# Output projection and FFN base layer as seven half-size products (Strassen's scheme) over two pairs of batch elements

## The chip, the core and the metric

The kernel runs on one core of a Trainium2 chip. A core has five engines with a queue each: TensorE (PE, with its weight loads shown apart as PEld), VectorE (DVE), ScalarE (ACT), GpSimd (POOL) and SyncE (SP), which here issues every DMA. Engines wait for each other through semaphores only, and each works through its own queue in order. The metric is the device time of one execution in microseconds (us).

## The reference, cut to what matters

```python
# x is [32, 64, 1024]: 2048 tokens of 1024 features; all in float32
x = x + attn(cond(x))                 # attn ends with: return y @ w_proj.T
c = conv1d(x)(9 taps, 4 groups) + ctx + bias
base   = c @ W_base.T + b_base
logits = c @ W_router.T               # 8 experts, the top 2 taken
h      = einsum('td,erd->ter', c, A)  # 8 experts x rank 16
lora   = einsum('ter,te,eor->to', h, w, B) * SCALING
x = x + base + lora
```

`cond` mixes the 64 channels of each batch element with weights that an MLP makes for it. Attention is over 64 tokens with 32 heads of 32, a causal mask and a ten-token prefix.

## The kernel before

Every wide product is done in FP32R, TensorE's one-pass form of float32. To keep the precision, each operand is split into a high and a low part (`hi` by a copy on ACT, `lo = raw - hi` by a subtraction on DVE), and a product is three passes: hi*hi, hi*lo, lo*hi (`split_passes`). The tokens are 16 pairs of batch elements (`NP`), 128 tokens each.

- **Attention** (`unit_step`) runs over 8 head groups `g` of 128 columns times 4 units `u` of 512 tokens, 32 units. In a unit `n = 4g + u` PE does the scores of the unit before (`attend_scores`, L774), turns that unit's values (`turn_values`, L834, which waits for `vT_copied`), projects K, Q and V (L822), turns the probabilities of the unit before between Q and V (`attend_transposes`, L783 and L790), and ends with `attend_values` of the unit before (L799, L805). DVE does the softmax of the unit before, the rotation of K and Q, and in a unit with `u == 0` three small operations that end in `avbd` (L1409), which waits for `attend_values` (`y_mm`). ACT copies V out of PSUM (`vT`, L1122) when V's projection is done. With `u == 3` the next group's q/k/v weights are split (`w_st`, `w_hi`, `w_lo`; L1020, L1189). The attention's output goes to DRAM (`y_scratch`).
- **Output and FFN stage** (`pair_step`) takes one pair after another. For a pair PE does the output projection of pair p+2 (`project_out`, L882: 8 chunks x 3 passes x 2 halves of 512 columns = 48 matmuls), the FFN's last layer of pair p (`last_layer`, L909: 8 x 3 x 3 = 72 matmuls of 388 or 384 columns, for 1024 base, 128 adapter and 8 router columns), a transpose (L919), the convolution of pair p+1 (`convolve`, L894: 16 matmuls in float32, 32 records), and the low-rank term (`low_rank`, L929: 9 matmuls). DVE adds the residual (L1283), puts the router together and writes the output; POOL adds the bias (L745). Between projection and convolution the pair goes through DRAM once (`x_scratch`, L672 and L681).
- The order on each engine is that of the code: written out by hand, with no scheduler. All weights of the stage are split once, near the end of attention (`wproj_hi`, `wffn_hi` and their `lo`).

## Time and profile before

| | us |
|---|---|
| median of 3 runs (lowest to highest) | 1203.87 (1201.65 to 1205.7) |
| the profiled execution | 1202.29 |
| its span | 1200.5 |
| PE busy | 1184.9 (99%) |
| DVE busy | 725.1 (60%) |
| ACT busy | 385.5 (32%) |
| POOL busy | 55.2 (5%) |
| DMA queue 1 | 84.32 MB, 20.9% of 16 engines |

The profile is of one execution, and its times count from the start of the span. Attention with its mixing stage takes the first 730 us or so, the output and FFN stage the rest. A busy share is an average over stages; a matmul's duration includes the time in which the next one already runs, so the pace of matmuls is read from the distance between starts, not from durations.

### The profile page before, as it was taken

The page shows a single profiled execution, that of the slowest core. Times are in us where ns is not written, and L with a number is a line of the kernel's source. Part 1 is how long each engine was busy: PE and PEld are TensorE (multiplying, and loading weights), DVE is VectorE, ACT ScalarE, POOL GpSimd, SP SyncE. Part 2 cuts the span into 40 slices and gives each one's busy share as a digit, 9 for nine tenths or more (in the row PEclk, how much of TensorE's full clock was granted, in tenths as well). Part 3 has the DMA queues.
Part 4 walks back from the last instruction along what each step waited for, and adds up shares of the span by engine and source line. Part 5 has one row for each costly group of instructions (what it writes and reads, how often), then busy time and mean ns, then how long its engine had stood idle before and what let it go on. Part 6 is the DMA issues. An engine that isn't in the chain of part 4 may idle for free.

```text
span 1200.5 us, 19493 instructions
## 1 busy us (share of the span) xinstructions
PE 1184.9 (99%) x7936; PEld 1032.0 (86%) x7936; DVE 725.1 (60%) x1484; ACT 385.5 (32%) x702; POOL 55.2 (5%) x25
## 2 busy tenths in 40 slices
PE   6999999999999999999999999999999999999998
PEld 5988888888888888888888888899999999999998
DVE  5887767677777777768768598633333333333333
...
PEclk9999999999999999999999999999999999999999
...
GB/s 255 126 37 70 10 19 62 10 19 62 20 9 68 13 9 72 9 12 69 9 57 24 150 97 187 126 90 90 91 90 90 92 107 92 91 90 90 108 73 54
DMA packets 58679, 85.56 MB, mean 71 GB/s; under 512 B 5963, under 2 KB 44767, under 8 KB 57695
## 3 DMA queue, kind: packets, MB, share of 16 engines
q1 hardware_dynamic: 58590, 84.32, 20.9%
...
## 4 chain that ended last, share of the span: by engine, by line
PE 96%; DVE 2%; issue 1%; POOL 0%; ACT 0%; SPq 0%; DMA 0%; DVEq 0%
PE psum L822 44%; PE psum L909 17%; PE psum L882 13%; PE psum L894 4%; PE psum L774 3%; PE psum L805 3%; PE psum L790 2%; PE psum L929 2%; PE psum L252 2%; PE psum L834 2%; PE psum L843 1%; PE psum L783 1%; PE psum L799 1%; DVE z L345 0%; POOL f_x1b L745 0%
## 5 line engine op out<-in xcount | busy, mean ns | idle before, releaser
L822 PE MATMUL psum<-z,w_hi 128*128 128x512 f32 x1536 | 481.7, 395 | 0.0
L822 PEld LDWEIGHTS psum<-z,w_hi 128*128 128x128 f32 x1536 | 282.4, 188 | 55.5
L822 PE MATMUL psum<-z,w_lo 128*128 128x512 f32 x768 | 300.1, 391 | 0.0
L822 PEld LDWEIGHTS psum<-z,w_lo 128*128 128x128 f32 x768 | 144.1, 188 | 31.5
L1091 ACT ACTIVATE a_kbd<-a_kr 32x512 f32<-32x512 f32 x128 | 80.8, 631 | 225.6 <-DVE a_kr L1207 224.5
L745 POOL TENSOR_TENSOR f_x1b<-f_x,_bbase 128x1024 f32<-128x1024 f32 x16 | 50.4, 3153 | 1072.8 <-DVE a_aprob L1257 690.3
L1221 DVE TENSOR_TENSOR a_prob<-psum,a_mask 128x512 f32<-128x512 f32 x64 | 44.0, 687 | 86.0 <-PE psum L774 86.0
L909 PE MATMUL psum<-f_wfhi,f_chi 128*128 128x384 f32 (+1 forms) x360 | 85.7, 339 | 0.6 <-DVE f_clo L1313 0.6
L909 PE MATMUL psum<-f_wflo,f_chi 128*128 128x384 f32 (+1 forms) x360 | 85.5, 338 | 0.0
L909 PE MATMUL psum<-f_wfhi,f_clo 128*128 128x384 f32 (+1 forms) x360 | 85.3, 338 | 0.0
L1327 DVE COPY f_lg<-psum 128x8 f32<-128x8 f32 x16 | 2.7, 168 | 130.2 <-PE psum L909 130.2
L882 PE MATMUL psum<-f_wphi,f_yhi 128*128 128x512 f32 x240 | 74.5, 391 | 0.7 <-ACT a_ysb L1040 0.7
L882 PE MATMUL psum<-f_wplo,f_yhi 128*128 128x512 f32 x240 | 74.2, 390 | 0.0
L882 PE MATMUL psum<-f_wphi,f_ylo 128*128 128x512 f32 x240 | 74.0, 390 | 0.0
L909 PEld LDWEIGHTS psum<-f_wfhi,f_chi 128*128 128x128 f32 x360 | 65.1, 188 | 2.1 <-issue 1.0
L1283 DVE TENSOR_TENSOR f_x<-psum,f_xt 128x1024 f32<-128x1024 f32 x14 | 28.8, 2054 | 63.0 <-PE psum L882 59.5
L909 PEld LDWEIGHTS psum<-f_wfhi,f_clo 128*128 128x128 f32 x360 | 64.9, 188 | 0.0
L909 PEld LDWEIGHTS psum<-f_wflo,f_chi 128*128 128x128 f32 x360 | 64.8, 188 | 0.0
L1073 ACT ACTIVATE f_rs<-f_rs 128x1 f32<-128x1 f32 x16 | 3.3, 204 | 179.8 <-DVE f_rs L1330 179.8
L894 PE MATMUL psum<-_toep,_x 128*128 128x128 f32 x512 | 59.8, 275 | 0.0
L1133 ACT ACTIVATE a_vbd<-psum 64x256 f32<-64x256 f32 x128 | 48.7, 381 | 33.8 <-PE psum L834 32.6
L894 PEld LDWEIGHTS psum<-_toep,_x 128*128 128x128 f32 x512 | 58.5, 192 | 1.2
...
## 6 DMA issues: line engine op xcount, KB each, us to landing
w_st<-in_wqkvT SPq DMA_DIRECT2D x7, 1536.0 KB, 6.9
m_x<-in_x SPq DMA_DIRECT2D x16, 512.0 KB, 4.2
y_scratch<-a_ysb SPq DMA_DIRECT2D x32, 256.0 KB, 2.5
f_yst<-y_scratch SPq DMA_DIRECT2D x16, 512.0 KB, 4.4
f_xt<-in_x SPq DMA_DIRECT2D x16, 512.0 KB, 3.6
x_scratch<-f_x SPq DMA_DIRECT2D x16, 512.0 KB, 2.6
_x<-x_scratch SPq DMA_DIRECT2D x128, 64.0 KB, 2.6
out<-f_osb SPq DMA_DIRECT2D x15, 512.0 KB, 2.8
```

The lines of the kernel that those rows point to most:

```text
L252: mm = pe.matmul(slot_bank(i, c // 4)[:, (c % 4) * P:(c % 4 + 1) * P], xbuf[i % NX][:, c * P:(c + 1) * P], aggT[:, i, :, :].rearrange("p b ...
L745: pool.tensor_tensor(x1b[:].rearrange("p (m q) -> p q m", q=PH), x1[:].rearrange("p (q m) -> p q m", q=PH), bbase[:].rearrange("p (m q) -> ...
L774: mm = pe.matmul(bS[2 * t + s // 2][NC * b:NC * b + NC, at:at + KW], qr[heads, (2 * s + b) * NC:(2 * s + b + 1) * NC], kbd[heads, 2 * s + ...
L805: mm = pe.matmul(y[2 * HD * hp:2 * HD * (hp + 1), (2 * s + b) * NC:(2 * s + b + 1) * NC], vbd[:, s, b, hp, :], pT[hp][:, s, NC * b:NC * b ...
L822: mm = pe.matmul(dst, w[:, c, x, :], zs, start=(c == 0 and i == 0), stop=(c == KC - 1 and i == 2))
L882: mm = pe.matmul(proj_banks(p)[n], y[:, c, :], w[:, c, n * 512:(n + 1) * 512], start=(c == 0 and i == 0), stop=(c == KC - 1 and i == 2))
L894: mm = pe.matmul(bC[:, o:o + P], x8[:, CONV * b + g, j:j + P], toep[:, g, j, :], start=(j == 0), stop=(j == 1))
L909: mm = pe.matmul(bF[:, at:at + n1 - n0], a[:, c, :], w[c][:, n0:n1], start=(c == 0 and i == 0), stop=(c == KC - 1 and i == 2))
L1091: cp = act.activation(kbd[HD * h:HD * (h + 1), :, h % 2 * NC:(h % 2 + 1) * NC], kr[HD * h:HD * (h + 1), :].rearrange("p (b k) -> p b k", k ...
L1133: cp = act.activation(vbd[NC * h:NC * (h + 1), :, b, :, HD * h:HD * (h + 1)], bV[NC * b:NC * (b + 1), :].rearrange("p (s a h e) -> p s a h ...
L1221: dve.tensor_tensor(prob[t][:].rearrange("p (s h) k -> p s h k", h=2), score_slots[:, UP * t:UP * (t + 1), 0:2 * NC].rearrange("p s (h k) ...
L1283: dve.tensor_tensor(x1[:].rearrange("p (q m) -> p m q", q=PH), bP.rearrange("p (m q) -> p m q", q=PH), xt[:].rearrange("p (m q) -> p m q", ...
```

## The change

Two pairs of batch elements (256 tokens) now make a group `G`. A product `Y = X W` of 256 tokens by 1024 by 1024 is cut into 2 x 2 blocks: X into blocks of 128 tokens by 512 features (A11, A12 of the first pair, A21, A22 of the second), W into blocks of 512 by 512. Strassen's scheme (in Winograd's form) makes the four blocks of Y from seven block products instead of eight: of A11, S1, A22, S2, A12, S4, S3, where S1 = A21+A22, S2 = S1-A11, S4 = A12-S2, S3 = A11-A21, with seven matching forms of W. Shares that several output blocks have in common are added by DVE (`shares`, `share21`, `share12`), or stay in the PSUM bank in which the next product adds to them.

- The stage has two phases: groups 0 to 7 do the output projection, groups 8 to 15 the FFN. Between them x plus bias goes through DRAM (`xn_scratch`). Groups 7 to 14 hold the two convolutions for the FFN group behind them.
- A product (`product`) is 4 chunks x 3 passes = 12 matmuls of 512 columns. The adapter and router columns (136 of them) are a product of their own (`hidden`, 2 pairs x 8 chunks x 3 passes = 48 matmuls of 136 columns), and the low-rank term is 12 matmuls of 512 columns.
- The seven forms of each weight matrix are made during attention: 16 preparations (`prep_at`), one in every unit with `u` 0 or 1 but the first, and one in unit 30. Each loads 1 MB of raw weights into the place of `w_st`, which is free then, makes four differences on DVE, splits seven parts of 256 columns (three copies on ACT, three subtractions on DVE), and stores 1.8 MB in `w_forms` in DRAM. A form in use (`wform`) is 2 MB; the four first ones are loaded in the last head group, the others behind it, and those of the FFN in group 7 (`turn_group`), each when group 7 has done the product that used its place.

The core of the diff:

```diff
 NF = L + NE * RANK + NE
+HALF, KH = L // 2, KC // 2
+NJ = NP // 2
+NPROD = 7
+A11, S1, A22, S2, A12, S4, S3, A21 = range(8)
+WEIGHT_SLOT = (0, 3, 4, 5, 1, 2, 6)
+B11, B21, B22, T1, T4, T2, T3 = range(NPROD)
+NPREP, PREP = 16, HALF // 2
...
-        def proj_banks(p):
-            return (bV, bQ) if p == 1 else (bQ, bK)
+            return bY if m < NG * NU - 1 else bS[3]
+        def prep_at(n):
+            g, u = n // NU, n % NU
+            if n == NG * NU - 2:
+                return NPREP - 1
...
+            def store_prep(k):
+                sp.wait_ge(prep_lo_set, 3 * (k + 1))
+                gemm, c, h = prep_part(k)
+                for part, s0, s1, src in ((0, 0, 5, prep_hi), (0, 5, 7, prep_hi_two), (1, 0, 7, prep_lo)):
+                    sp.dma_start(w_forms[gemm, s0:s1, :, part, c, PREP * h:PREP * (h + 1)].rearrange("s p n -> p s n"),
+                                 src[:].bitcast(F32)).then_inc(prep_out, 16)
+                sp.wait_ge(prep_out, 48 * (k + 1))
+            def load_form(gemm, i):
+                if gemm:
+                    sp.wait_ge(prod, NPROD * (NJ - 1) + i + 1)
+                sp.dma_start(wform[i][:].bitcast(F32), w_forms[gemm, WEIGHT_SLOT[i]]).then_inc(wform_in[i], 16)
...
             def unit_step(g, u):
+                n = NU * g + u
+                if n and prep_at(n - 1) is not None:
+                    store_prep(prep_at(n - 1))
+                if prep_at(n) is not None:
+                    load_prep(prep_at(n), u == 0 or n == 1)
                 if last(g):
...
+            def put_aside(G, t):
+                row_ready(G, t)
+                sp.dma_start(x1_dram[2 * G + t], x1[:, t, :]).then_inc(x1_out[t], 16)
+            def keep(G, t):
+                sp.wait_ge(xn_set, 2 * G + t + 1)
+                sp.dma_start(xn_dram[2 * G + t], xn[:, t, :]).then_inc(xn_out[t], 16)
...
+                load_ctx(p)
+                sp.wait_ge(x1_out[p % 2], 16 * (p // 2 + 1))
+                wait(sp, conv_mm, 2 * (p - 1) if p >= 2 else 0)
...
+            def turn_group():
+                G = NJ - 1
+                put_aside(G - 1, 0)
+                put_aside(G - 1, 1)
+                load_form(1, 0)
+                keep(G - 1, 0)
+                load_form(1, 1)
+                keep(G - 1, 1)
+                load_form(1, 2)
+                load_form(1, 3)
+                spread(2)
+                load_form(1, 4)
+                spread(3)
+                load_form(1, 5)
+                put_aside(G, 0)
+                load_form(1, 6)
+                put_aside(G, 1)
+                keep(G, 0)
+                load_x(G + 1, 0)
+                keep(G, 1)
+                load_x(G + 1, 1)
...
+            def product(G, i):
+                if G % NJ == 0:
+                    pe.wait_ge(wform_in[i], 16 * (G // NJ + 1))
+                pe.wait_ge(act_set, form_count(low_order, i, G))
+                if i == 0:
+                    wait(pe, row1_set, 2 * G - 1 if G else 0)
+                if i == 1:
+                    wait(pe, row1_set, 2 * G)
+                if i == 2:
+                    wait(pe, u21_set, G)
+                if i == 3:
+                    wait(pe, row2_set, G)
+                if i == 4:
+                    pe.wait_ge(s1_set, G + 1)
+                if i == 5:
+                    pe.wait_ge(u22_set, G + 1)
+                if i == 6:
+                    pe.wait_ge(w12_set, G + 1)
+                for c in range(KH):
+                    for n, (a, w) in enumerate(split_passes(act_hi[i], act_lo[i], 0, 1)):
+                        mm = pe.matmul(prod_bank[i][:], a[:, c, :], wform[i][:, w, c, :],
+                                       start=(i < 4 and c == 0 and n == 0), stop=(c == KH - 1 and n == 2),
+                                       skip_group_check=True)
+                mm.then_inc(prod, 1)
...
+            def hidden(G):
+                j = G - NJ
+                if j == 0:
+                    pe.wait_ge(wh_lo, 1)
+                wait(pe, hw_set, j)
+                for t, halves in enumerate(((A11, A12), (A21, A22))):
+                    for half, f in enumerate(halves):
+                        pe.wait_ge(act_set, form_count(low_order, f, G))
+                        for c in range(KH):
+                            for n, (a, w) in enumerate(split_passes(act_hi[f], act_lo[f], whhi, whlo)):
+                                mm = pe.matmul(bH[:, HIDDEN * t:HIDDEN * (t + 1)], a[:, c, :], w[:, KH * half + c, :],
+                                               start=(half == 0 and c == 0 and n == 0),
+                                               stop=(half == 1 and c == KH - 1 and n == 2))
+                mm.then_inc(hidden_mm, 1)
...
+            def group(G):
+                if ffn(G):
+                    hidden(G)
+                for i in range(4):
+                    product(G, i)
+                if ffn(G):
+                    turn_hidden(G)
+                if NJ - 1 <= G < 2 * NJ - 1:
+                    convolve(2 * (G - NJ + 1))
+                product(G, 4)
+                if NJ - 1 <= G < 2 * NJ - 1:
+                    convolve(2 * (G - NJ + 1) + 1)
+                product(G, 5)
+                if ffn(G):
+                    if G == NJ:
+                        pe.wait_ge(lora_lo, 1)
+                    pe.wait_ge(hwT_set, G - NJ + 1)
+                    low_rank(G, bA, 0, 0)
+                    low_rank(G, bC, 0, 1)
+                    low_rank(G, bD, 1, 2)
+                    pe.wait_ge(w12_set, G + 1)
+                    low_rank(G, bB, 1, 1)
+                product(G, 6)
+            for G in range(1, 2 * NJ):
+                group(G)
...
+            def prep_high(k):
+                act.wait_ge(prep_in, 32 * (k + 1))
+                wait(act, prep_out, 48 * k)
+                act.activation(prep_hi[:, 0:3, :], prep_raw[:, 0:3, :], ACT.Copy).then_inc(prep_hi_set, 1)
+                act.wait_ge(prep_sum, 4 * (k + 1))
+                act.activation(prep_hi[:, 3:5, :], prep_raw[:, 3:5, :], ACT.Copy).then_inc(prep_hi_set, 1)
+                act.activation(prep_hi_two[:], prep_raw[:, 5:7, :], ACT.Copy).then_inc(prep_hi_set, 1)
...
+            def first_share(G):
+                act.wait_ge(prod, NPROD * G + 1)
+                wait(act, v2_set, G)
+                act.activation(s1[:], bA[:], ACT.Copy).then_inc(s1_set, 1)
...
+                if prep_at(n) is not None:
+                    prep_high(prep_at(n))
+                if n == NG * NU - 1:
+                    for f in form_order(0):
+                        high(0, f)
                 act.wait_ge(mm_done[V_], n + 1)
                 wait(act, v_tr, n)
                 act.activation(vT[:], bV[:], ACT.Copy).then_inc(vT_copied, 1)
...
+            def prep(k):
+                dve.wait_ge(prep_in, 32 * (k + 1))
+                part = prep_raw
+                def take(dst, a, b, done):
+                    wait(dve, prep_sum, done)
+                    dve.tensor_tensor(part[:, dst, :], part[:, a, :], part[:, b, :], ALU.subtract).then_inc(prep_sum, 1)
+                take(T3, B22, T1, 0)
+                take(T1, T1, B11, 0)
+                take(T2, B22, T1, 4 * k + 2)
+                take(T4, B21, T2, 4 * k + 3)
+                for n, (s0, s1_, hi) in enumerate(((0, 3, prep_hi[:, 0:3, :]), (3, 5, prep_hi[:, 3:5, :]),
+                                                   (5, 7, prep_hi_two[:]))):
+                    dve.wait_ge(prep_sum, 4 * (k + 1))
+                    dve.wait_ge(prep_hi_set, 3 * k + n + 1)
+                    dve.tensor_tensor(prep_lo[:, s0:s1_, :], prep_raw[:, s0:s1_, :], hi.bitcast(F32), ALU.subtract
+                                      ).then_inc(prep_lo_set, 1)
...
+            def shares(G):
+                dve.wait_ge(s1_set, G + 1)
+                dve.wait_ge(x_in[0], 16 * (G + 1))
+                dve.tensor_tensor(w12[:], s1[:], x_of(G, 0)[:, HALF:L], ALU.add)
+                dve.wait_ge(x_in[1], 16 * (G + 1))
+                dve.tensor_tensor(u2[:], x_of(G, 1).rearrange("p (s n) -> p s n", s=2),
+                                  s1[:].rearrange("p (s n) -> p s n", s=1).broadcast_to([P, 2, HALF]), ALU.add
+                                  ).then_inc(v2_set, 1)
+                dve.wait_ge(v2_set, G + 1)
+                dve.wait_ge(prod, NPROD * G + 2)
+                dve.tensor_tensor(u2[:, 1, :], bC[:], u2[:, 1, :], ALU.add).then_inc(u22_set, 1)
...
+            def out_half(G, t, half, src, other):
...
                     dve.wait_ge(conv_mm, 2 * p + b + 1)
                     dve.tensor_tensor(
...
+                        raw[:, t, :, NC * b:NC * (b + 1)].rearrange("p q (g o) -> p g q o", g=CONV),
+                        bConv[:, 512 * b:512 * (b + 1)].rearrange("p (g q o) -> p g q o", g=CONV, q=PH),
+                        ctxb[t][:, b * NC:(b + 1) * NC].rearrange("p (g a o) -> p g a o", g=CONV, a=1)
                         .broadcast_to([P, CONV, PH, CG]), ALU.add).then_inc(conv_set, 1)
...
+                if prep_at(n) is not None:
+                    prep(prep_at(n))
+                if n == NG * NU - 1:
+                    first_forms()
...
+            def group(G):
+                if G:
+                    row2(G - 1)
+                    add_up(G, S3)
+                    low(G, S3)
+                if ffn(G):
+                    router(G)
+                shares(G)
+                if not ffn(G):
+                    share21(G)
+                if G < NJ - 1:
...
+                elif G < 2 * NJ - 1:
+                    share12(G)
+                    if ffn(G):
+                        split_hidden(G)
+                    convolved(2 * (G + 1 - NJ))
+                    low(G + 1, A11)
+                    low(G + 1, A12)
+                    convolved(2 * (G + 1 - NJ) + 1)
+                    low(G + 1, A22)
+                    low(G + 1, A21)
+                    add_up(G + 1, S1)
+                    add_up(G + 1, S2)
+                    low(G + 1, S1)
+                    out11(G)
+                    out12(G)
+                    if ffn(G):
+                        share21(G)
+                    add_up(G + 1, S4)
+                    low(G + 1, S2)
+                    low(G + 1, S4)
                 else:
-                    finish_last()
-                if ahead >= 2:
```

**ACT in a unit with `u == 0` (unit 4).** Before, in program order, from the copy of the turned probabilities to that of V's values (`a_vT`, `a_ysb` the attention's output, `a_vbd` V's blocks):

```order
L1032 ACTIVATE a_aT<-psum 128x512 [waits a_y_mm,a_a_tr]
L1035 ACTIVATE a_pT_106<-psum 128x512 [waits a_p_tr]
L1035 ACTIVATE a_pT_107<-psum 128x512 [waits a_p_tr]
L1114 ACTIVATE a_kbd<-psum 32x8x10 [waits a_scores,a_ak_tr]
L1114 ACTIVATE a_kbd<-psum 32x8x10 x3
L1122 ACTIVATE a_vT<-psum 128x512 [waits a_v_tr,a_v_mm]
L1040 ACTIVATE a_ysb<-psum 128x512 [waits a_y_out,a_y_mm]
L1133 ACTIVATE a_vbd<-psum 64x4x2x32 [waits a_y_mm,a_v_tr]
```

Now, the same place:

```order
L1146 ACTIVATE a_aT<-psum 128x512 [waits a_y_mm,a_a_tr]
L1149 ACTIVATE a_pT_110<-psum 128x512 [waits a_p_tr]
L1149 ACTIVATE a_pT_111<-psum 128x512 [waits a_p_tr]
L1223 ACTIVATE a_kbd<-psum 32x8x10 [waits a_scores,a_ak_tr]
L1223 ACTIVATE a_kbd<-psum 32x8x10 x3
L1160 ACTIVATE f_prep_hi<-f_prep_raw 128x768 [waits f_prep_out,f_prep_in]
L1162 ACTIVATE f_prep_hi<-f_prep_raw 128x512 [waits f_prep_sum]
L1163 ACTIVATE a_prep_hi_two<-f_prep_raw 128x512
L1236 ACTIVATE a_vT<-psum 128x512 [waits a_v_tr,a_v_mm]
L1154 ACTIVATE a_ysb<-psum 128x512 [waits a_y_out,a_y_mm]
L1247 ACTIVATE a_vbd<-psum 64x4x2x32 [waits a_y_mm,a_v_tr]
```

The three `prep` copies stand ahead of the copy of V, and the second of them waits for `prep_sum`, which DVE raises in four differences behind `avbd`.

**SP where the phases meet.** Before, in the stage's steady step (`f_yst` and `f_xt` are the inputs of a pair, `_x` the convolution's):

```order
L636 DMA f_xt<-in_x 128x1024 [waits f_x1_set]
L632 DMA f_yst<-y_scratch 128x1024 [waits f_y_lo]
L693 DMA out<-f_osb 128x1024 [waits f_out_set]
L628 DMA a_ctxb_122<-ctx_scratch 128x128 [waits f_conv_set]
L672 DMA x_scratch<-f_x_80 128x1024 [waits f_x1_set]
L681 DMA _x_91<-x_scratch 16x8x128 [waits f_conv_mm,f_x1_out]
L681 DMA _x_91<-x_scratch 16x8x128 x7
L636 DMA f_xt<-in_x 128x1024 [waits f_x1_set]
L632 DMA f_yst<-y_scratch 128x1024 [waits f_y_lo]
```

Now, from the load of the fifth FFN form in `turn_group` (`f_wform_53`) on; `x_scratch` takes x, `xn_scratch` takes x plus bias, `f_xn` is read back for FFN group 8:

```order
L682 DMA f_wform_53<-w_forms 128x4096 [waits f_prod]
L703 DMA f_ctxb_136<-ctx_scratch 128x128 [waits f_conv_set]
L760 DMA f_x_next<-x_scratch 16x8x128 [waits f_conv_mm,f_x1_out1]
L760 DMA f_x_next<-x_scratch 16x8x128 x7
L682 DMA f_wform_54<-w_forms 128x4096 [waits f_prod]
L746 DMA x_scratch<-f_x_126 128x1024 [waits f_row1]
L682 DMA f_wform_55<-w_forms 128x4096 [waits f_prod]
L746 DMA x_scratch<-f_x_126 128x1024 [waits f_row2]
L750 DMA xn_scratch<-f_xn 128x1024 [waits f_xn_set]
L699 DMA f_xn<-xn_scratch 128x1024 [waits f_row1,f_xn_out0]
L750 DMA xn_scratch<-f_xn 128x1024 [waits f_xn_set]
L699 DMA f_xn<-xn_scratch 128x1024 [waits f_v2,f_xn_out1] x2
```

Seven loads of 2 MB have come into the queue between the stores of the projection, and the reads of `f_xn` for group 8 wait for a store of `xn_scratch` to have landed.

**DVE in FFN group 8.** Behind the router, in program order (`f_w_84` and `f_u_85` hold the shares, `f_raw` the convolution's output, `f_act_lo` the low parts for group 9):

```order
L1428 TENSOR_TENSOR f_w_84<-f_s_83,f_xn 128x512 [waits f_x_in0,f_s1]
L1430 TENSOR_TENSOR f_u_85<-f_xn,f_s_83 128x1024 [waits f_x_in1]
L1435 TENSOR_TENSOR f_u_85<-psum,f_u_85 128x512 [waits f_prod,f_v2]
L1448 TENSOR_TENSOR f_w_84<-psum,f_w_84 128x512 [waits f_v2,f_prod]
L1547 TENSOR_TENSOR f_hwTlo<-psum,f_hwThi 128x256 [waits f_hwT_hi]
L1494 TENSOR_TENSOR f_raw<-psum,f_ctxb_135 128x4x8x16 [waits f_conv_mm,f_ctxb_in0]
L1494 TENSOR_TENSOR f_raw<-psum,f_ctxb_135 128x4x8x16 [waits f_conv_mm]
L1422 TENSOR_TENSOR f_act_lo_64<-f_raw,f_act_hi_56 128x512 [waits f_act_hi]
L1422 TENSOR_TENSOR f_act_lo_68<-f_raw,f_act_hi_60 128x512 [waits f_act_hi]
L1494 TENSOR_TENSOR f_raw<-psum,f_ctxb_136 128x4x8x16 [waits f_conv_mm,f_ctxb_in1]
L1494 TENSOR_TENSOR f_raw<-psum,f_ctxb_136 128x4x8x16 [waits f_conv_mm]
```

Before, this engine's convolution output stood behind the router with nothing between that waited for a DMA but `a_ctxb`. Now it stands behind two additions that wait for `x_in0` and `x_in1`, and the second convolution of a group on PE waits for the first one's output (`conv_set`).

## Rows read from the trace of the kernel before

**Rows 1.** The page: busy time, and the span in 40 slices.
```profile
PE 1184.9 (99%) x7936; PEld 1032.0 (86%) x7936; DVE 725.1 (60%) x1484; ACT 385.5 (32%) x702; POOL 55.2 (5%) x25
PEclk9999999999999999999999999999999999999999
```
**Rows 2.** Whom PE waited for: total us, times, longest.
```profile
PE psum L774 <- DVE a_avs L1404: 1.1, 1, 1.1
PE psum L882 <- ACT a_ysb L1040: 0.7, 1, 0.7
PE psum L909 <- DVE f_clo L1313: 0.6, 1, 0.6
```
**Rows 3.** Timeline of PE, one pair of the stage: start us, us, instruction.
```profile
906.46 0.69 PE L909 MATMUL psum<-f_wfhi,f_chi 128*128 128x384 f32 x3
...
919.14 0.63 PE L882 MATMUL psum<-f_wphi,f_yhi 128*128 128x512 f32 x2
...
923.37 3.73 PE L894 MATMUL psum<-_toep,_x 128*128 128x128 f32 x32
926.86 0.36 PE L929 MATMUL psum<-f_loraBhi,f_hwThi 128*128 128x248 f32 x1
927.06 0.28 PE L929 MATMUL psum<-f_loraBlo,f_hwThi 128*128 128x248 f32 x1
927.18 0.28 PE L929 MATMUL psum<-f_loraBhi,f_hwTlo 128*128 128x248 f32 x1
927.29 0.34 PE L929 MATMUL psum<-f_loraBhi,f_hwThi 128*128 128x388 f32 x1
...
928.34 0.63 PE L882 MATMUL psum<-f_wphi,f_yhi 128*128 128x512 f32 x2
```
**Rows 4.** Timeline of PE, in the pair before it.
```profile
899.64 0.62 PE L882 MATMUL psum<-f_wphi,f_yhi 128*128 128x512 f32 x2
```
**Rows 5.** Timeline of PE, end of unit 16 and unit 17.
```profile
410.92 1.24 PE L774 MATMUL psum<-a_kbd,a_qr 64*64 64x148 f32 x32
412.08 0.65 PE L834 MATMUL psum<-_ident,a_vT 128*128 128x128 f32 x4
423.50 0.60 PE L783 MATMUL psum<-_ident,a_aprob 128*128 128x128 f32 x4
```
**Rows 6.** Timeline of DVE there.
```profile
411.10 0.29 DVE L1409 TENSOR_TENSOR a_avbd<-a_avs,a_avh 128x128 fp32r<-128x128 f32 x1 [2.73 <-PE psum L805]
412.20 0.69 DVE L1221 TENSOR_TENSOR a_prob<-psum,a_mask 128x512 f32<-128x512 f32 x1 [0.81 <-PE psum L774]
416.66 0.33 DVE L1232 TENSOR_TENSOR a_atmp<-psum,a_astat 128x160 f32<-128x160 f32 x1
421.80 0.24 DVE L1257 CAST a_aprob<-a_aprob 128x160 fp32r<-128x160 f32 x1
433.00 0.69 DVE L1221 TENSOR_TENSOR a_prob<-psum,a_mask 128x512 f32<-128x512 f32 x1 [5.36 <-PE psum L774]
```
**Rows 7.** Timeline of ACT, units 16 and 17.
```profile
409.71 0.60 ACT L1122 ACTIVATE a_vT<-psum 128x512 f32<-128x512 f32 x1 [1.99 <-PE psum L822]
427.86 1.08 ACT L1035 ACTIVATE a_pT<-psum 128x512 f32<-128x512 f32 x2
```
**Rows 8.** DMA issues: what, times, KB each, median us from issue to landing.
```profile
w_st<-in_wqkvT SPq DMA_DIRECT2D x7, 1536.0 KB, 6.9
y_scratch<-a_ysb SPq DMA_DIRECT2D x32, 256.0 KB, 2.5
f_xt<-in_x SPq DMA_DIRECT2D x16, 512.0 KB, 3.6
out<-f_osb SPq DMA_DIRECT2D x15, 512.0 KB, 2.8
```
**Rows 9.** The loads of `f_wp_raw` (8 of 512 KB): issue on SP, landing.
```profile
L643 SPq DMA_DIRECT2D f_wp_raw<-in_wprojT x8: 432/448/876, 669.6 to 673.7; - x8
DMA to landing us min/median/max: 4.2/6.8/9.4
```
**Rows 10.** Timeline of DVE, the last operation.
```profile
1197.20 0.56 DVE L1372 TENSOR_TENSOR f_osb<-psum,f_x1b 128x388 f32<-128x388 f32 x1 [2.09 <-PE psum L929]
```

More of the change, by code:

```diff
@@ L391, in program, with at @@
[L391 to L395 removed]
+        FORM = 2 * KH * HALF * 4
+        def at(name, place, shape, dt=F32):
+            return Space(nc, "f", place).take(name, shape, dt)
+        acts_at, staged_at = zbase + 2 * Z, zbase + NU * Z
+        wide_at = staged_at + KC * 3 * P * 4
@@ new lines, in ffn_group @@
+            def ffn_group(G):
+                if G > NJ:
+                    store_out(G - 1, 1)
+                if G < 2 * NJ - 1:
+                    load_x(G + 1, 1)
+                if G < 2 * NJ - 2:
+                    spread(2 * (G - NJ + 2))
+                    spread(2 * (G - NJ + 2) + 1)
+                if G < 2 * NJ - 1:
+                    load_x(G + 1, 0)
+                store_out(G, 0)
+            for G in range(NJ - 1):
+                proj_group(G)
+            turn_group()
@@ L1453, in build @@
+            for G in range(2 * NJ):
+                group(G)
+ROUTE_EXP, ROUTE_ALL = 4, 16
 def build(nc, d, out):
```

805 lines of the change are left out of this document (393 added, 412 removed).

## The prediction

> **What bounds the kernel now.** I read the page first: PE is busy 99% of the span, and its granted clock is at full speed in all 40 slices, the higher of its two levels, 2.4 GHz [rows 1]. Then the waits of PE: behind the first 70 us they are single waits of about 1 us or less [rows 2]. So the path is PE's own queue, and what counts is the number of matmuls times their pace. The other question is whether DVE, ACT or SP, none of them full, now makes PE wait.
>
> Pace, from distances between starts: the last 30 matmuls of a projection take 906.46 - 899.64 = 6.82 us, 0.227 us for one of 512 columns [rows 3, 4]. The 72 of the last layer take 919.14 - 906.46 = 12.68 us (0.176 each). A low-rank matmul of 248 columns takes 0.115 (927.06 to 927.29 is two), all nine 1.48 (926.86 to 928.34), a convolution 926.86 - 923.37 = 3.49 [rows 3].
>
> **The change part by part.**
>
> *Matmuls, in 8 x two pairs.* Projection: 96 of 512 columns become 84: -12 x 0.227 = -2.7 us. FFN before: 2 x (12.68 + 1.48) = 28.3. After: 84 x 0.227 = 19.1, low rank 12 x 0.227 = 2.7, hidden columns 48 x (136 columns), together 21.8 + hidden. No row has a single pass of 136 columns. Lower bound: by columns from the 248-column row, 0.115 x 136/248 = 0.063. Upper bound: as slow per column as the float32 convolution, 3.49/16 = 0.218 for 128 columns, so 0.232. The nearest row is 248 columns at 0.115, and I take it: 48 x 0.115 = 5.5, FFN after 27.3, gain 1.0. Convolutions and transposes are the same. Sum: 8 x (2.7 + 1.0) = -29.7 us, with bounds of the hidden columns at -20 and +45 around it.
>
> That 248 columns take 0.115 where 136/248 would leave half says nothing yet of a floor. The Trainium skill (TensorE: Matmul & The Clock Gate, LDWEIGHTS) gives a weight load as its columns over 1.2 GHz, 107 ns for 128: by that the hidden matmuls go at 0.107 or more. The same page (Back-to-back issue gap) states about 81 ns for a sustained pair of load and matmul at 128 columns: by that hidden is 3.9 us a group, and the sum 13 us lower. The rows cannot tell these two apart.
>
> *Preparation in units with u = 0.* Seven of them (head groups 1 to 7). DVE's four differences stand behind `avbd`, which waits for the unit's last PE work and ends at 411.39 [rows 6]. One of 256 columns: between 0.33 (160 columns) and 0.69 (512) by column 0.43; the second does not depend on the first (0.34 from start to start), the others do: they end at about 413.1. ACT then makes two copies of 512 columns (two take 1.08, [rows 7]) and only then V's copy, 0.60. Without them V's copy is at 409.71, without a wait on PE's side. Now it ends near 413.1 + 1.0 + 0.6 = 414.8. PE turns the values at 412.08 [rows 5], and waits from there: 2.7 us. Queued behind it are K's, Q's and V's projections; nothing covers it. The three low-part subtractions (about 2.2 us) follow on DVE, so the softmax starts at 415.1 instead of 412.20, 2.9 later; since PE is 2.7 late itself and had 423.50 - 422.04 = 1.5 us to spare at the probabilities [rows 5, 6], nothing is added. Price 7 x 2.7 = 18.9. Bounds: 2.2 each (differences overlapping) to 3.2.
>
> *Preparation in units with u = 1 (8) and unit 30.* DVE is idle 5.36 us before the next softmax [rows 6], the work is 3.9. ACT is free from 428.9 [rows 7]. Hidden, cost 0, as long as the raw weights have landed: SP stores 1.8 MB in 1 KB pieces, waits for it to land, then loads 1 MB. At the pace of the single large load, 1.57 MB in 6.9 us less a fixed 1.6 (`y_scratch`: 0.26 MB in 2.5, so 1.6 fixed at 0.3 MB/us, [rows 8]), 0.3 MB/us, that is 7.7 + 5.1 us from 415 on, landing near 428; needed at about 430.5. Two us more per unit and V's copy is late: up to +16.
>
> *End of attention.* The first group's forms, 2.8 us of sums and 4.6 of low parts on DVE, push the last softmax to about its limit; there are the same four or five short waits as before [rows 2]. +1, between -1 and +4. The forms 4 to 6 land before they are used.
>
> *Projection groups.* PE 84 x 0.227 = 19.1 us. DVE, by operations of 512 columns at 0.65 to 0.98, 15.3, and no wait of PE has less than 1.5 us to spare. DMA is 4.2 MB in 19.1 us. Cost 0.
>
> *The turn, groups 7 and 8.* Time from the start of group 7. PE: group 7 with two convolutions lasts 26.1. Group 8: hidden to 31.6, products 0 to 3 to 42.5, transposes and a convolution to 46.4, product 4 to 49.1, then the second convolution. That waits for `conv_set` of the first, DVE's work behind `shares(8)`, which waits for x of both pairs from `xn_scratch`. SP issues these reads last in `turn_group`, each behind a store that must have landed, and the queue ahead holds from 2.7 us on seven forms of 2.1 MB, three stores and two spreads of 0.5 MB, some 17 MB. Rate: eight queued loads of 0.52 MB took from 669.6 to 673.7 + 9.4 = 683.1 [rows 9]; less the fixed 1.6 that is 4.19 / 11.9 = 0.35 MB/us; I take 0.365, since the first issues were not queued. Form 6 ends at 52, the store of group 7's last x and of `xn` at 55, landed 56.7; read x0 (3.6, [rows 8]) 60.4, store, landed 61, read x1 64.6. Then DVE: shares, one hidden part and the convolution's output, 4.6: 69.2. PE waits 69.2 - 49.1 = 20 us. Bounds: at 0.41 MB/us 15, at the single load's 0.30 30; and 0, if a small store does not have to wait behind the forms. The landing times of rows 9, from 4.2 for the shortest to 9.4, the more that is queued, speak for one queue in order; I take 20. The Trainium skill (DMA: Bandwidth & Descriptors, Queues, rings and completion order) says that on each DMA engine the descriptors of a ring are consumed in order, which rows 9 bear out.
>
> After 20 us without work PE may come back at the lower clock, 1.2 GHz; no row shows it there. Nothing to one convolution's 3.5 us; I take half, 1.7.
>
> *FFN groups 9 to 15.* 34.8 us each on PE; DVE's chain (router, shares, two convolution outputs, four low parts) ends about 5 us ahead of the next hidden product. Cost 0.
>
> *The end.* Before, one subtraction of 388 columns, 0.56 [rows 10], and a store of part of a row. Now two additions of 512 columns (1.3 us) and a store of 512 KB, 2.8 [rows 8]: 1.3 + 2.8 = 4.1 against 1200.5 - 1197.2 = 3.3, so +0.8; with the longer issue I take +1 (0 to 1.5).
>
> *Sum* against the profiled execution, 1202.3 (span 1200.5 and 1.8 around it): -29.7 + 18.9 + 1 + 20 + 1.7 + 1 = +12.9, 1215.2. The median of the runs shown is 1.6 above that execution: 1216.8, **1217 us**.
>
> **The rivals.**
> - *The small stores and reads pass the forms (or these move faster), so that the turn costs nothing.* Then 1217 - 21.7 = 1195.5. For it: the DMA engines are at a fifth of their time over the span. Against it: rows 9. 10%.
> - *V's copy is not held up, only the turn is.* 1217 - 18.9 = 1198. Against it: ACT works in order, and the order rows have the copies ahead. 5%. Neither of the two: 1177, 7%.
> - *The hidden columns go by the column, at 0.063 (the 248-column row scaled), or between that and 0.115*: up to 48 x 8 x 0.052 = 20 us less, 1197, 12%; half of it on the faster side. The other way, at 0.232: 1262, 4%. By the 81 ns that the Trainium skill's TensorE page (Back-to-back issue gap) states it would be 1204.
> - *The weights in 1 KB pieces come late in the units with u = 1*: 8 x 1.8 = +14, 1231, 9%. The price starts once store and load together take over 16 us.
> - That the change does not do what it says is not a case: seven products of 12 matmuls stand in the order.
>
> **How the numbers follow.** The forecast has 50%, its own range 1209 to 1229; the last 3% is spread. What this kernel's measurement can tell from no change is about 0.3%, 3.6 us. Faster than 1200.3: the turn free alone, neither wait, V's copy free alone and half of the fast hidden columns, 10 + 7 + 5 + 6 = 28%. Within: 8%, the other half and the low edge of the forecast. Slower: 64%. The range from 1193 to 1234 leaves out the case with neither wait, the slow hidden columns and some of the tails.
>
> **What would show it.** In the profile after: about 84 matmuls of 512 columns per group at 0.227; L999 in place of L882 and L909; the distance of the hidden matmuls, 0.115; seven waits of PE at the turning of V, 2.7 us each, on ACT's copy, none with u = 1; one wait of some 20 us of PE ahead of a convolution in FFN group 8, with DVE idle on a DMA to `f_xn` and the DMA engines full for 50 us before it; no PE wait over 1 us in groups 1 to 6 and 9 to 15. The forecast is wrong if the seven waits are below 1 us, if `f_xn` lands before product 4 of group 8 ends, or if PE waits in each group.

## The result, and the profile after

| | before | after |
|---|---|---|
| median, us (lowest to highest, 4 runs each) | 1204.78 (1201.65 to 1207.39) | 1247.12 (1242.56 to 1252.09) |
| the profiled execution, its span | 1202.29, 1200.5 | 1246.03, 1244.2 |
| mean granted clock | 1.000 | 0.979 |

The change makes the kernel slower: ratio 1.0353, 95% interval 1.0305 to 1.0402. The forecast was slower too, but 1217 us with a range up to 1234, 30 us short.

The page after, against [rows 1]: fewer matmuls, but PE is no longer full, and its clock is not either. In the slice from 964 to 995 us, PE and the clock drop together:

```profile
PE 1171.9 (94%) x7696; PEld 986.9 (79%) x7696; DVE 926.2 (74%) x1741; ACT 440.8 (35%) x807; POOL 59.4 (5%) x25
...
PE   7999999999999999999999999798999199999998
...
PEclk9999999999999999999999999899999599999999
...
DMA  7413132041041232222231587676579624334311
```

Whom PE waited for, which had no entry over 1.1 us behind the first 70 us [rows 2] (total us, times, longest):

```profile
PE psum L1014 <- DVE f_raw L1494: 26.1, 1, 26.1
PE psum L942 <- ACT a_vT L1236: 19.2, 8, 2.7
PE psum L999 <- DVE f_w L1448: 6.8, 1, 6.8
...
PE psum L999 <- DVE f_x L1462: 2.7, 2, 2.4
PE psum L999 <- DVE f_u L1435: 2.4, 4, 0.9
```

A ledger by stage comes from starts of PE instructions. The scores of a unit (L774, now L882) start at 67.47 and, for unit 30, at 710.10 before; at 70.89 and 736.20 after. The span ends at 1200.5 and 1244.2.

| stage | before | after | difference | forecast |
|---|---|---|---|---|
| start, to the first scores | 67.5 | 70.9 | +3.4 | 0 |
| attention, to the scores of unit 30 | 642.6 | 665.3 | +22.7 | +18.9 |
| from there to the end | 490.4 | 508.0 | +17.6 | -6.0 |

In the last stage the distance from product 0 of one group to product 0 of the next gives the group lengths (84 matmuls of 0.227 are 19.1). The right column is the last kernel of this study (e7), which has the same matmuls and, but for 2.5 us in group 0, no wait there:

| group | after | e7 |
|---|---|---|
| 0, with the end of attention | 31.4 | 25.1 |
| 1 to 6, each | 19.1, 19.9, 20.8, 23.3, 20.3, 20.4 | 19.0 |
| 8, the turn | 63.7 | 34.7 |
| 9 to 14, each | 34.7 | 34.7 |

So 8.8 us are lost in group 0 (against 25.1 - 2.5 = 22.6), 9.5 in groups 1 to 6, 29.1 in the turn: 47.4. What is left is 17.6 - 47.4 = -29.8 us, the size forecast for the matmuls. The steady steps give it directly: before, one pair took 28.70 us (899.64 to 928.34, [rows 3, 4]), so two took 57.4; now a projection group and an FFN group take 19.0 + 34.7 = 53.7, and 8 x 3.7 is 29.6.

**The turn.** SyncE, then VectorE, then PE (start us, us, instruction):

```profile
957.47 0.43 SPq L682 DMA_DIRECT2D f_wform<-w_forms  x1
957.95 0.43 SPq L746 DMA_DIRECT2D x_scratch<-f_x  x1
958.42 0.43 SPq L750 DMA_DIRECT2D xn_scratch<-f_xn  x1
977.10 0.32 SPq L699 DMA_DIRECT2D f_xn<-xn_scratch  x1
```
```profile
981.25 0.69 DVE L1428 TENSOR_TENSOR f_w<-f_s,f_xn 128x512 f32<-128x512 f32 x1 [25.52 <-DMA f_xn<-xn_scratch]
985.76 1.23 DVE L1430 TENSOR_TENSOR f_u<-f_xn,f_s 128x1024 f32<-128x1024 f32 x1 [3.82 <-DMA f_xn<-xn_scratch]
```
```profile
989.98 6.10 PE L1014 MATMUL psum<-_toep,f_x_next 128*128 128x128 f32 x32 [26.06 <-DVE f_raw L1494]
```

A store of 0.5 MB that stands behind forms 5 and 6 takes 18.7 us to land (958.42 to 977.10, where SyncE's wait for it ends), where a load or store of that size took 2.8 to 3.6 [rows 8]. Only then may `f_xn` be loaded for group 8. The convolution behind the wait takes 6.10 us instead of 3.73 [rows 3]: the windows of PE (us, busy, granted clock, DMA share, GB/s) show the lower clock level, 1.2 GHz, from within the wait until nearly 5 us behind it.

```profile
963.00:966.00 3.00, 0.93 (x5) 1.00 0.93 393
966.00:970.00 4.00, 0.00 (x0) 0.69 1.04 438
970.00:975.00 5.00, 0.00 (x0) 0.50 0.93 388
...
990.00:994.00 4.00, 4.00 (x19) 0.50 0.44 111
994.00:998.00 4.00, 4.00 (x25) 0.90 0.18 40
```

**Groups 1 to 6.** GpSimd and VectorE in group 2:

```profile
810.19 3.40 POOL L854 TENSOR_TENSOR f_xn<-f_x,_bbase 128x1024 f32<-128x1024 f32 x1 [10.33 <-DVE f_x L1462]
817.00 3.43 POOL L854 TENSOR_TENSOR f_xn<-f_x,_bbase 128x1024 f32<-128x1024 f32 x1 [3.42 <-DVE f_x L1462]
```
```profile
809.94 0.68 DVE L1414 TENSOR_TENSOR f_act_sum<-f_raw,f_act_sum 128x512 f32<-128x512 f32 x1
810.54 4.19 DVE L1422 TENSOR_TENSOR f_act_lo<-f_act_sum,f_act_hi 128x512 fp32r<-128x512 f32 x2
...
814.92 2.01 DVE L1462 TENSOR_TENSOR f_x<-psum,f_u 128x512 f32<-128x512 f32 x2
816.77 0.68 DVE L1416 TENSOR_TENSOR f_act_sum<-f_raw 128x512 f32<-128x512 f32 x1
818.20 2.78 DVE L1422 TENSOR_TENSOR f_act_lo<-f_act_sum,f_act_hi 128x512 fp32r<-128x512 f32 x1 [0.76 <-ACT f_act_hi L1181]
```

The operation that was running when GpSimd began (809.94) is not stretched. One low part behind it is: it ends 0.55 us behind GpSimd's end (820.43 and 820.98). Beside each of the 16 additions there is exactly one such low part, and it ends 0.54 or 0.55 us behind the addition, whenever it began: it did not run slowly, it stood still. The two in a group cost VectorE 2.9 + 2.1 = 5 us. VectorE is busy, or stopped, for 18.7, 19.9 and 22.1 us of groups 2, 3 and 4, where PE's 84 matmuls take 19.1, and so PE waits. All 64 of this form, in ns (least, median, longest), with first and last start:

```profile
L1422 DVE TENSOR_TENSOR f_act_lo<-f_act_sum,f_act_hi x64: 677/693/3681, 756.5 to 1215.3; 128x512 fp32r<-128x512 f32 x64
```

In the kernel before, the same addition fell into an idle time of VectorE, two rows of its trace:

```profile
902.21 3.10 POOL L745 TENSOR_TENSOR f_x1b<-f_x,_bbase 128x1024 f32<-128x1024 f32 x1 [25.61 <-DVE f_osb L1361]
```
```profile
906.66 2.07 DVE L1283 TENSOR_TENSOR f_x<-psum,f_xt 128x1024 f32<-128x1024 f32 x1 [4.59 <-PE psum L882]
```

**Group 0.** The low parts of group 1 stand ahead of `share12(0)`, for which product (0,6) waits, and they wait for the load of the attention output (`f_raw`). SyncE had issued it only at 776.73, behind forms 4 to 6 and the last `y` store. That store could not go sooner, as ScalarE copied its values at 775.64:

```profile
759.41 1.48 SPq L682 DMA_DIRECT2D f_wform<-w_forms  x3
776.27 0.37 SPq L657 DMA_DIRECT2D y_scratch<-a_ysb  x1
776.73 0.45 SPq L687 DMA_DIRECT2D f_raw<-y_scratch  x1
```

```profile
783.29 1.29 DVE L1422 TENSOR_TENSOR f_act_lo<-f_raw,f_act_hi 128x512 fp32r<-128x512 f32 x2 [10.31 <-ACT f_act_hi L1181]
784.50 0.68 DVE L1448 TENSOR_TENSOR f_w<-psum,f_w 128x512 f32<-128x512 f32 x1
```
```profile
785.33 1.19 PE L999 MATMUL psum<-f_wform,f_act_hi 128*128 128x512 f32 x2 [6.79 <-DVE f_w L1448]
```

### The profile page after: what moved, and what is told of

Read it like the earlier page. It is cut to its first block, busy times and chain, and to the rows that moved or that the text cites. A ratio compares the mean times of both kernels' runs of the same rounds, so it can differ in the third digit from the quotient of the medians.

```text
span 1244.2 us, 19823 instructions
## 1 busy us (share of the span) xinstructions
PE 1171.9 (94%) x7696; PEld 986.9 (79%) x7696; DVE 926.2 (74%) x1741; ACT 440.8 (35%) x807; POOL 59.4 (5%) x25
## 4 chain that ended last, share of the span: by engine, by line
PE 81%; DVE 8%; DMA 5%; issue 3%; ACT 2%; SPq 0%; DVEq 0%; ACTq 0%
PE psum L930 41%; PE psum L999 16%; PE psum L1014 5%; PE psum L1028 3%; PE psum L913 3%; DMA f_raw<-y_scratch 2%; PE psum L260 2%; PE psum L882 2%; PE psum L898 2%; DMA xn_scratch<-f_xn 2%; PE psum L1045 2%; DVE f_x L1462 2%; PE psum L942 2%; PE psum L951 1%; PE psum L891 1%
## 5 line engine op out<-in xcount | busy, mean ns | idle before, releaser
L999 PE MATMUL psum<-f_wform,f_act_hi 128*128 128x512 f32 x896 | 282.7, 397 | 12.3 <-DVE f_w L1448 6.8
L999 PEld LDWEIGHTS psum<-f_wform,f_act_hi 128*128 128x128 f32 x896 | 167.0, 190 | 50.2 <-issue 16.3
L999 PE MATMUL psum<-f_wform,f_act_lo 128*128 128x512 f32 x448 | 176.0, 393 | 0.0
L999 PEld LDWEIGHTS psum<-f_wform,f_act_lo 128*128 128x128 f32 x448 | 85.1, 190 | 18.5
L854 POOL TENSOR_TENSOR f_xn<-f_x,_bbase 128x1024 f32<-128x1024 f32 x16 | 54.6, 3411 | 829.9 <-DVE f_x L1462 829.9
L1422 DVE TENSOR_TENSOR f_act_lo<-f_act_sum,f_act_hi 128x512 fp32r<-128x512 f32 x64 | 83.2, 1312 | 12.6 <-ACT f_act_hi L1181 12.5
L1139 ACT ACTIVATE a_prob<-a_prob 128x512 f32<-128x512 f32 x64 | 40.5, 633 | 52.8 <-DVE a_prob L1347 51.8
L1014 PE MATMUL psum<-_toep,f_x_next 128*128 128x128 f32 x256 | 32.3, 288 | 26.1 <-DVE f_raw L1494 26.1
L1322 DVE STREAM_SHUFFLE a_rot<-psum 128x512 f32<-128x512 f32 x64 | 47.0, 734 | 0.0
L1347 DVE TENSOR_TENSOR a_prob<-a_prob,a_stat 128x512 f32<-128x512 f32 x64 | 44.3, 692 | 2.2
L1325 DVE TENSOR_TENSOR a_rot<-a_rot,a_sin 128x512 f32<-128x512 f32 x64 | 44.3, 692 | 2.2
## 6 DMA issues: line engine op xcount, KB each, us to landing
f_wform<-w_forms SPq DMA_DIRECT2D x14, 2048.0 KB, 14.2
```

Of the source, the lines that this page charges most:

```text
L854: pool.tensor_tensor(xn[:, t, :].rearrange("p (m q) -> p q m", q=PH), x1[:, t, :].rearrange("p (q m) -> p q m", q=PH), bbase[:].rearrange( ...
L999: mm = pe.matmul(prod_bank[i][:], a[:, c, :], wform[i][:, w, c, :], start=(i < 4 and c == 0 and n == 0), stop=(c == KH - 1 and n == 2), sk ...
L1014: mm = pe.matmul(bConv[:, o:o + P], x8[p % 2][:, CONV * b + g, j:j + P], toep[:, g, j, :], start=(j == 0), stop=(j == 1))
L1322: dve.stream_shuffle(rot[:], src[:], HALF_SWAP).then_inc(turned[x], 1)
L1325: dve.tensor_tensor(r, r, tab[1], ALU.mult).then_inc(rot_step, 1)
L1347: dve.tensor_tensor(prob[t][:], prob[t][:], spread(t, 0), ALU.subtract).then_inc(shifted, 1)
```

## The experiments

e1 to e8 are the changed kernel with an edit, given here in short; ratios are to the kernel before, which ran beside them, and a time "less" is against the changed kernel's 1247.12.

**e1, the order of SyncE's queue at the turn.**

```diff
-spread(2); load_form(1, 4); spread(3); load_form(1, 5); put_aside(G, 0); load_form(1, 6)
-put_aside(G, 1); keep(G, 0); load_x(G + 1, 0); keep(G, 1); load_x(G + 1, 1)
+spread(2); spread(3); put_aside(G, 0); keep(G, 0); load_form(1, 4); put_aside(G, 1); keep(G, 1)
+load_x(G + 1, 0); load_x(G + 1, 1); load_form(1, 5); load_form(1, 6)
```

> Edit: in the SyncE order of the turn (groups 7 and 8) both convolution loads, then the stores of x plus bias of group 7 and the loads of group 8's first xn come ahead of the last two FFN weight forms (5 and 6) instead of behind them. Nothing else changes. Theory A (order in the queue): the first xn of group 8 waited only behind 4 to 6 MB of forms that were issued earlier; the PE wait of 26.1 us at L1014 goes, with the stretch at half clock behind it (about 2.4 us), group 8 takes 35 us from its first product to the next group's instead of 64, and the time is 1218 us (1214 to 1222). Rival B (volume): the forms, two convolution inputs, stores and loads need the bandwidth in any order, so the wait moves to forms 5 or 6 (a wait of product 5 or 6 on f_wform) and at most half is gained: 1232 to 1247 us.

Measured: 1232.64 us, ratio 1.0229 (1.0206 to 1.0252), 14.5 less than the changed kernel; group 8 takes 49.0 us.

```profile
PE psum L1014 <- DVE f_raw L1494: 6.2, 1, 6.2
PE psum L999 <- DMA f_wform<-w_forms: 4.7, 1, 4.7
```

Half of each theory: the order made the wait as long as it was, and the volume sets what is left. Of the wait for x 6.2 us remain, and 4.7 us are new, a wait of product 4 for its form.

**e2, ScalarE's V copy ahead of two preparation copies (u = 0).**

```diff
 prep_high(k):       # now the first copy only
+# behind y_copy, in units with u == 0:
+prep_high_rest(k)   # the second and third copy
```

> Edit: in the units with u = 0 ScalarE does the second and third high copy of the weight preparation behind the copies of V and y instead of ahead of them. Theory A: the seven PE waits of 2.7 us at the turning of V (L942) came from these two copies, which themselves wait for VectorE; they go, with the three or so stretches at half clock behind them (1.7 us each): 18.8 + 5 = 24 us less, 1223 us (1219 to 1227). Rival B: VectorE's low parts of the preparation now come later, the softmax of the next unit is queued behind them, and PE waits at the transposes of the probabilities or at the next rotation instead: the wait at L942 is gone but the time falls by less than 10 us (1237 to 1247).

Measured: 1232.91 us, ratio 1.0220 (1.0192 to 1.0249), 14.2 less. The wait at L942 is gone, and this one is new:

```profile
PE psum L891 <- DVE a_aprob L1384: 9.5, 7, 1.5
```

Neither number was met; the mechanism is B's. PE no longer waits for VectorE's preparation, but the next softmax does. In one of the seven units it begins 4.2 us behind the start of PE's scores (424.18 and 419.99), where that was 1.3 [rows 5, 6], and PE waits 1.3 to 1.5 us for it at the transposes. The 1.5 us to spare that the forecast had read [rows 5, 6] was right, and is all there is.

**e3, the bias added by VectorE.**

```diff
-pool.tensor_tensor(xn..., x1..., bbase..., ALU.add)
+dve.tensor_tensor(xn..., x1..., bbase..., ALU.add)   # ahead of out11 of the next group
```

> Edit: the addition of the bias to x (16 times 128x1024, GpSimd's only work in the projection groups) is done by VectorE ahead of out11, so that GpSimd is idle. Theory A (GpSimd and VectorE exclude each other): the low parts that read two SBUF tiles (L1422) take 0.69 us each again, none over 1 us; the 16 additions cost VectorE about 1.3 us each, less than what they stretched, so groups 1 to 6 fall from 19.1 to 23.3 us towards 19.1 to 19.8, and the time by 5 to 12 us, 1235 to 1242. Rival B (the stretched ones are slow because of the DMA traffic, or because they write in place over their source): L1422 keeps its instances of 2.6 to 3.7 us, VectorE gets 2.6 us more work a group, and the groups take 21 to 24 us: 1250 to 1260.

Measured: 1273.89 us, ratio 1.0576 (1.0551 to 1.0601), 27 slower. Groups of instructions on VectorE (count, busy us, mean ns, idle before):

```profile
L1409 DVE TENSOR_TENSOR f_act_lo<-f_act_sum,f_act_hi 128x512 fp32r<-128x512 f32 x64 | 44.1, 691 | 14.0 <-ACT f_act_hi L1168 13.8
...
L1480 DVE TENSOR_TENSOR f_xn<-f_x,_bbase 128x1024 f32<-128x1024 f32 x16 | 33.1, 2114 | 0.1
```

Theory A's mechanism holds: with GpSimd idle the mean is 691 ns, where it was 1312 after, under the same DMA traffic and with the same writing in place, so B's causes are out. Its time was wrong. The addition takes 2.11 us on VectorE, not the 1.3 expected. Ahead of `out11`, two of them make PE wait 12.3 us for `f_x` in all; x plus bias is also stored later, and group 8 took 76 us.

**e4, the attention output of group 1 loaded first.**

```diff
 sp.wait_ge(mm_done[V_], NU * NG)
+sp.wait_ge(act_set, 4)
+load_y(1)
 for i in range(4, NPROD): load_form(0, i)
```

> Edit: SyncE loads the attention output of group 1 (1 MB) as soon as group 0's low parts have read the buffer, ahead of the projection's forms 4 to 6 and of the store of the last unit's output, instead of behind them. Theory A: the wait of 6.8 us ahead of product (0,6) goes (it stood behind the low parts of group 1 in VectorE's queue, which waited for this load) with the half clock behind it (1.8 to 2.2 us): 9 us less, 1238 us (1234 to 1242). Rival B: the forms now land 3 us later and product (0,4) or (0,5) waits for one of them, so less than 4 us is gained (1243 to 1248).

Measured: 1236.53 us, ratio 1.0254 (1.0232 to 1.0276), 10.6 less. The wait of 6.8 us is gone, at the price of waits of 3.3 us in all for forms; theory A. The edit puts the load ahead of the forms and of the `y` store at once; how much of the delay each had made, no run separates.

**e5, VectorE's preparation in two gaps (u = 0).**

```diff
 if u == 0:
+    prep_sums(k)                  # four differences
     ... avs, avh
+    prep_lows(k)                  # three low parts
     ... avbd
-prep(k)
```

> Edit: in the units with u = 0 VectorE makes the four differences of the weight preparation ahead of the adapter's values (avs) and its three low parts between avh and avbd, in gaps where it had been waiting 2.9 and 2.7 us, instead of behind all of them. ScalarE's order stays as in the changed kernel. Theory A (what made PE wait at the turning of V was when VectorE began the preparation): ScalarE's high copies are done before V is projected, both the waits at L942 and the ones that e2 put in their place at the transposes go, and all 24 us (18.8 of waits, about 5 of clock) are gained: 1223 us (1219 to 1227), PE waits of under 1 us in total in units 1 to 31 beside the 1.1 at the scores. Rival B (VectorE has no room in a unit with u = 0): the preparation in front pushes avbd or the next softmax back, PE waits at attend_values or the transposes, and no more is gained than in e2: 1231 to 1240.

Measured: 1222.09 us, ratio 1.0126 (1.0101 to 1.0151), 25.0 less. No wait at the transposes, 0.3 us at L942. VectorE's gap ahead of `avbd`, 2.73 us in [rows 6], is now filled:

```profile
412.27 0.29 DVE L1597 TENSOR_SCALAR a_avh<-a_avs,a_alow 128x128 fp32r<-128x128 f32 x1
412.89 1.56 DVE L1398 TENSOR_TENSOR f_prep_lo<-f_prep_raw,f_prep_hi 128x768 fp32r<-128x768 f32 x2 [0.33 <-ACT f_prep_hi L1160]
414.37 0.68 DVE L1398 TENSOR_TENSOR f_prep_lo<-f_prep_raw,a_prep_hi_two 128x512 fp32r<-128x512 f32 x1
415.30 0.29 DVE L1602 TENSOR_TENSOR a_avbd<-a_avs,a_avh 128x128 fp32r<-128x128 f32 x1 [0.25 <-PE psum L913]
```

Attention takes 641.5 us between the two marks of the ledger, 1 less than before: all of its loss was the place of this work, and none the work itself or its 45 MB of transfers.

**e6, the bias added in the FFN groups.**

```diff
-load_x of group 8..15 from xn_scratch (x plus bias), behind the stores of it
+load_x of group 8..15 from x_scratch (x); group 8's at the start of the turn; xn_scratch is gone
-pool: xn = x1 + bias, in groups 0..7
+pool: xn = xn + bias in place, in groups 8..15
```

> Edit: the projection groups no longer make x plus bias. GpSimd adds the bias in place in the FFN groups, to the x that is loaded from the first scratch tensor for the residual; VectorE reads it with a stride there; the second scratch tensor and its 8 MB of stores are gone, and group 8's x is loaded at the start of the turn, before the FFN forms. Theory A: (1) without GpSimd in the projection groups the low parts at 1.3 us fall to 0.69 and groups 1 to 6 lose 8 to 10 us in sum; (2) the turn's wait of 26.1 us and its 2.4 us of half clock go, since nothing of group 8 stands behind the forms any more; (3) in the FFN groups VectorE has some 10 us of idle time in 34.7, so that being stopped by GpSimd twice for up to 3 us costs nothing. Sum -37 us: 1210 us (1205 to 1215). Rival B: volume again, as in e1: product 5 or 6 of group 8 waits 4 to 8 us for forms; or GpSimd's additions stop VectorE ahead of a low part that PE waits for in every FFN group (7 x 1 to 3 us more): 1215 to 1235.

Measured: 1204.93 us, ratio 0.9988 (0.9974 to 1.0001), 42.2 less. Groups 1 to 6 sum to 114.3 us (123.7 after), group 8 takes 34.6. GpSimd still meets VectorE, which is busy for 24.2 of 34.7 us there, and PE does not feel it. Theory A on all three points; the edit changes all three at once, but e3 and e8 show GpSimd's part by itself and e1 half of the queue's. The meeting also shows which operations stop: one with two operands in SBUF does, also when it is not a low part (L1405 makes S3 from two parts of `f_raw`), and one that takes an operand from PSUM does not.

```profile
1072.35 2.94 POOL L852 TENSOR_TENSOR f_xn<-f_xn,_bbase 128x1024 f32<-128x1024 f32 x1 [17.02 <-DMA f_xn<-x_scratch]
1087.03 2.87 POOL L852 TENSOR_TENSOR f_xn<-f_xn,_bbase 128x1024 f32<-128x1024 f32 x1 [11.73 <-DMA f_xn<-x_scratch]
```
```profile
1072.79 3.05 DVE L1405 TENSOR_TENSOR f_act_sum<-f_raw 128x512 f32<-128x512 f32 x1
...
1087.16 0.69 DVE L1447 TENSOR_TENSOR f_w<-psum,f_w 128x512 f32<-128x512 f32 x1 [2.78 <-PE psum L988]
```

**e7, e4 + e5 + e6.**

> The edits of e4, e5 and e6 together. Theory A (the causes are separate and add): 1247 - 10.6 (e4's) - 24 - 37 = 1175 us (1170 to 1185), 2 to 3% under the kernel before, which is the size that the removed matmuls were worth (-29.7 us). Rival B (they share one limit, such as DMA volume or clock, so that the sum is not reached): 1190 to 1210.

Measured: 1174.09 us, ratio 0.9742 (0.9726 to 0.9757). This beats the kernel before by 31 us; the three gains would add to 77.8, and it has 73.0. The page:

```profile
PE 1157.7 (99%) x7696; PEld 979.3 (83%) x7696; DVE 921.8 (78%) x1749; ACT 440.5 (37%) x807; POOL 51.9 (4%) x25
...
PEclk9999999999999999999999999999999999999999
```

**e8, GpSimd writes but does not read.**

```diff
-pool.tensor_tensor(xn..., x1..., bbase..., ALU.add)
+pool.memset(xn..., 0.0)
```

> Edit: GpSimd writes zeros over the tile of x plus bias (a memset with the same stride) instead of adding x and bias; it reads nothing. This leaves out the bias and the residual of the FFN's output; all waits, stores and loads stay. Theory A (what GpSimd and VectorE share is needed by VectorE's operations with two tiles from SBUF, for reading, so only a GpSimd operation that reads stops them): the low parts are at 0.69 us in mean, even where they lie beside the memset; groups 1 to 6 at 19.0 to 19.3 us; 1237 us (1234 to 1241), as 10 us of group time go. Rival B (any GpSimd operation stops VectorE, or the buffer of the output is the cause): low parts beside a memset are stretched until it ends, as before, by its length.

Measured: 1230.24 us, ratio 1.0216 (1.0177 to 1.0255). One of the memsets, and a low part beside it:

```profile
814.35 2.12 POOL L854 MEMSET f_xn<- 128x1024 f32 x1 [2.06 <-DVE f_x L1460]
```
```profile
815.57 0.69 DVE L1420 TENSOR_TENSOR f_act_lo<-f_act_sum,f_act_hi 128x512 fp32r<-128x512 f32 x1 [0.76 <-ACT f_act_hi L1179]
```

The longest of the 64 is 696 ns, groups 1 to 6 take 19.0 to 19.1 us, and VectorE is busy for 14.8, 15.1 and 16.0 us of groups 2, 3 and 4. The stores are all still there, so they are not what held VectorE up. Theory A; the time is 7 us under its 1237, for the turn's wait is 21.4 us here: the memset is shorter (2.1 us), and `xn` can be stored sooner.

**e9 and e10, both kernels once more.**

> The kernel before, unchanged, for a second profile. In its profile the scores of the first unit start at 67.5 us, in those of the seven changed kernels at 68.6 to 72.5 us. Theory A (it varies between executions with the time at which the input lands): 69 to 72 us here. Rival B (the changed kernels start later for a reason of their own): 67 to 68 us again.

> The changed kernel, unchanged, for a second profile. Theory A: the five causes show again with the same sizes: seven waits of 2.7 us at the turning of V, one of 6 to 8 us in group 0, groups 1 to 6 at 19.1 to 23.5 us, one of 25 to 27 us at the convolution of the turn; the start between 68 and 73 us. Rival B: one of them was an accident of the first profile and is missing.

Measured: 1204.2 us with the first scores at 69.35, and 1248.82 us with them at 72.83; the waits of the latter are 25.7, 19.2 (8 times) and 6.4 us, its groups 1 to 6 are 19.1 to 23.4 us long. All of them show again, so none was an accident of the first profile. The start varies by execution (67.5 and 69.4 before, 68.6 to 72.8 in the ten changed ones), PE waiting 1.2 to 4.8 us for the input there. The two pairs differ by 3.4 and 3.5 us, but the ranges overlap. Whether any of it is the change's stays open.

## Why the prediction was wrong

The sum was +12.9 us on the profiled execution; it came out at +43.7. By its steps:

- *Matmuls, -29.7*: right. With the end of attention and the tail it is -27.7, and the ledger leaves -29.8. Every third hidden matmul of a group:

```profile
L1028 PE MATMUL psum<-f_whhi,f_act_lo x16: 270/275/277, 1039.0 to 1044.0; 128*128 128x136 f32 x16
```

  45 steps in 5.0 us are 0.111 each; 0.115 was taken. Of the Trainium skill's two figures (TensorE: Matmul & The Clock Gate), the weight load of 107 ns (LDWEIGHTS) agrees as a floor, and the 81 ns a pair (Back-to-back issue gap) does not.
- *Preparation with u = 0, +18.9*: right in place, count and size (2.69 us each). Not priced: about the end of three of the seven waits (160.53, 250.58 and 517.61) the granted clock falls to its lower level, 1.2 GHz, so that it is 0.66 in the mean of the 5 us from 160.5, 250.5 and 516.9 on; behind the other four it stays at 1.00. Windows of PE (us, busy, granted clock, DMA share, GB/s), for two of the three and one of the four:

```profile
160.50:165.50 5.00, 4.97 (x17) 0.66 0.73 233
250.50:255.50 5.00, 4.92 (x17) 0.66 0.73 231
340.60:345.60 5.00, 4.92 (x24) 1.00 0.73 231
```

  That is 1.7 us lost each time, 5.1 in all. Attention lost 22.7, 3.8 more than forecast; without waits it is about 1 us shorter than before, as e5 shows.

- *Preparation with u = 1 and unit 30, 0*: right; e5 shows no wait there.
- *Projection groups, 0*: wrong, +9.5. "DVE, by operations of 512 columns at 0.65 to 0.98, 15.3, and no wait of PE has less than 1.5 us to spare" counted VectorE's operations at their lengths alone. That sum is right where nothing stops them (14.8 to 16.0 in e8). It left out that two of GpSimd's additions now fall among them, which stop an operation with two SBUF operands until they end, 5 us a group. e3 and e8 show it, e6 gives it back.
- *End of attention, +1*: wrong, +8.8 in group 0. "The forms 4 to 6 land before they are used" asked only about the forms. It did not ask what stands behind them in SyncE's queue: the load of group 1's input, with a store ahead of it that had to wait for its own values. e4 shows it.
- *The turn, +21.7*: right mechanism, mis-sized, 29.1. The wait began where the sum had it (963.9; 914.05 + 49.1 is 963.2) and was 26.1 us long, not 20. The queue moved 336, 295 and 266 GB/s in the stretches 917 to 946, 946 to 955 and 955 to 963, and 406 from there to 975; over the whole it is 334, not 365, which makes 5 of the 6 us for the sum's 19 MB (an estimate: 19.1 MB at 0.334 against 0.365 MB/us). The half clock was priced at 1.7 and costs 2.4.

```profile
917.00:975.00 58.00, 46.67 (x279) 0.94 0.95 334
```

- *FFN groups, 0*: right, 34.67 us from one to the next in groups 9 to 14, with no wait.
- The start, +3.4, is open.

Unforeseen: 9.5 + 8.8 + 7.4 + 3.8 + 3.4 - 2.1 = 30.8, the gap. Three fifths of it are waits that the sum had at nothing after looking at one engine or one transfer alone. None of the rivals came true, since each varied a part that the sum had looked at; none had GpSimd or the order behind the forms in it.
